# A graph attention layer and a graph network with pair features: the first weight turned alone, the other weights after the first graph, and the layer norm of thirty graphs placed between the steps of the last two

## The reference, cut to what matters

```python
# x (32, 256, 128), adj (32, 256, 256); layer norms are without gain and bias
def _L0_gnn_ref(x, adj, W, b, a):            # H = 4 heads of D = 32
    h = (x @ W + b).reshape(Bb, Nn, H, D)
    e_i = jnp.einsum('bnhd,d->bnh', h, a_i)
    e_j = jnp.einsum('bnhd,d->bnh', h, a_j)
    e = e_i[:, :, None, :] + e_j[:, None, :, :]
    e = jnp.where(e > 0, e, 0.2 * e)
    e = jnp.where(adj[..., None] > 0, e, NEG)
    attn = jax.nn.softmax(e, axis=2)
    return jnp.einsum('bijh,bjhd->bihd', attn, h).reshape(Bb, Nn, H * D)
...
x = _layernorm(x + _L0_gnn_ref(x, adj, ...), axis=-1)
x = _layernorm(x + _L1_gnn_ref(x, adj, W1, ..., Wg, ..., Wt, ...), axis=-1)
```

## Time and profile before

| | before |
|---|---|
| time of the runs | median 2240.56 us of 3 (2239.26 to 2241.79) |
| profiled execution | 2237.45 us, its span 2235.6 us |
| DVE busy | 2090.6 us, 94% |
| ACT busy | 2093.6 us, 94% |
| PE busy | 1977.0 us, 88% |
| granted PE clock, mean | 0.984 of full |

### The profile page before, as it was taken

One profiled execution on the slowest core, in us unless ns is written; L12 is line 12 of the kernel. 1 busy time (PEld: TensorE's weight loads), 2 busy tenths in 40 slices (PEclk: granted clock), 3 DMA queues, 4 the chain that ended last, 5 costly groups with the idle time before them and its releaser, 6 DMA issues.

```text
span 2235.6 us, 35341 instructions
## 1 busy us (share of the span) xinstructions
PE 1977.0 (88%) x13059; PEld 781.5 (35%) x13059; DVE 2090.6 (94%) x2519; ACT 2093.6 (94%) x2764; POOL 54.6 (2%) x50
## 2 busy tenths in 40 slices
PE   6888878989989898989899898986999999999986
PEld 4666533333333333333333333332222222222225
DVE  6999789999999999999999999998899999999976
ACT  4999879999999999999999999996999999999976
POOL 0000000000000000000000000000000000111000
PEclk9999989999999999999999999998999999999997
DMA  4112144445444444444454444444999999999972
GB/s 127 51 51 58 30 155 183 174 182 193 179 177 182 180 176 189 186 184 173 184 190 181 178 178 187 174 184 170 370 348 359 365 369 361 372 357 367 362 258 76
DMA packets 221281, 470.52 MB, mean 210 GB/s; under 512 B 52344, under 2 KB 143288, under 8 KB 196536
## 3 DMA queue, kind: packets, MB, share of 16 engines
q1 hardware_dynamic: 220048, 467.91, 56.4%
q10 hardware_dynamic: 1064, 0.36, 0.1%
HBM read 254.25 MB, written 213.91 MB: 209 GB/s over the span
## 4 chain that ended last, share of the span: by engine, by line
ACT 38%; DVE 22%; issue 21%; PE 4%; DMA 2%; SPq 1%; POOL 0%; ACTq 0%; POOLq 0%; DVEq 0%
DVE diff L1334 10%; ACT hcopy L625 9%; ACT habs L625 9%; ACT yt L630 8%; ACT diff L613 7%; DVE diff L1339 4%; ACT banks L635 2%; PE banks L863 1%; ACT diff L615 1%; ACT habs L657 1%; DVE adjt L1351 1%; DMA hcopy<-kept 1%; DVE small L1364 1%; DVE rows L1179 1%; DMA diff<-kept 1%
## 5 line engine op out<-in xcount | busy, mean ns | idle before, releaser
L863 PE MATMUL banks<-diff,w1t 128*64 128x512 f32 x5136 | 1206.6, 603 | 128.6 <-ACT hcopy L625 57.0
L1194 DVE TENSOR_TENSOR diff<-ring 128x2048 f32<-128x2048 f32 x352 | 802.9, 2289 | 42.0 <-PE banks L863 42.0
L863 PEld LDWEIGHTS banks<-diff,w1t 128*64 128x64 f32 x5136 | 346.5, 137 | 862.5 <-issue 792.8
L1208 DVE TENSOR_SCALAR diff<-diff 128x2048 int32<-128x2048 int32 x354 | 418.5, 1221 | 0.0
L1334 DVE TENSOR_TENSOR diff<-ring 128x2048 f32<-128x2048 f32 x128 | 296.1, 2313 | 3.5 <-PE banks L863 3.5
L613 ACT ACTIVATE diff<-banks 128x2048 f32<-128x2048 f32 x128 | 238.5, 1863 | 2.7 <-PE banks L878 2.7
L630 ACT ACTIVATE yt<-habs,par 128x2048 f32<-128x2048 f32 x96 | 192.4, 2005 | 3.1
L630 ACT ACTIVATE yt<-hcopy,par 128x2048 f32<-128x2048 f32 x96 | 192.4, 2005 | 3.1
L625 ACT ACTIVATE hcopy<-banks 128x1024 f32<-128x1024 f32 x192 | 193.7, 1018 | 0.6 <-PE banks L863 0.6
L625 ACT ACTIVATE habs<-banks 128x1024 f32<-128x1024 f32 x192 | 193.7, 1018 | 0.3 <-PE banks L863 0.3
L878 PE MATMUL banks<-pick,yt 32*128 32x256 f32 x2560 | 184.9, 403 | 1.0 <-ACT ring L596 1.0
(11 more groups left out here) (213 smaller groups left out, 1852.1 us busy)
## 6 DMA issues: line engine op xcount, KB each, us to landing
kept<-hcopy SPq DMA_DIRECT2D x192, 512.0 KB, 2.9
kept<-habs SPq DMA_DIRECT2D x192, 512.0 KB, 2.9
hcopy<-kept SPq DMA_DIRECT2D x78, 1024.0 KB, 6.9
diff<-kept SPq DMA_DIRECT2D x76, 1024.0 KB, 7.0
habs<-kept SPq DMA_DIRECT2D x38, 1024.0 KB, 7.0
yt<-xrows SPq DMA_DIRECT2D x512, 40.0 KB, 2.0
adjt<-in_adj_dram SPq DMA_DIRECT2D x32, 256.0 KB, 2.9
diff<-in_x_dram SPq DMA_DIRECT2D x32, 128.0 KB, 2.1
```

The costliest lines, as they stand in the source:

```text
L863: last = nc.tensor.matmul(dst[half * O:(half + 1) * O, bank * BANK:(bank + 1) * BANK], w1t[:, :], src[:, m * BANK:(m + 1) * BANK], start=T ...
L1194: v.tensor_tensor(shaped(diff[:, c % ND, :]), xj, xi_, ALU.subtract).then_inc(sub_done, 1)
L1208: v.tensor_scalar(bits, bits, ABS_BITS, None, ALU.bitwise_and).then_inc(abs_dve, 1)
```

## The change

Three things. **Start:** W0 alone is turned first, and `v` goes to the PSUM bank 6 instead of bank 2, so that PE can turn the first x without waiting for DVE's copy of `v`; SP takes over one column of `a` and the loads of W1, Wg and Wt; these are turned (`turn_weights`) and copied (`keep_weights`) after the first graph's scores. SP no longer waits for W1, Wg and Wt ahead of the rows' load. **End:** moments, square root and reciprocal of the 60 tiles of graphs 0 to 29 are taken while graphs 30 and 31 drain, groups 0 to 4 are scaled there, and the last four tiles get moments of their own. **Place:** `em` and `pt` lie further back in `ring`, since its front is now filled while they are in use, and the turned groups go to PSUM banks 0, 1, 6 and 7.

```diff
-        em = [ring[:, q * 2048:(q + 1) * 2048] for q in range(2)]
-        pt = ring[:, 8192:8192 + NT * H * N].rearrange("p (t h n) -> p t h n", t=NT, h=H)
+        em = [ring[:, 6144 + q * 2048:6144 + (q + 1) * 2048] for q in range(2)]
+        pt = ring[:, 10240:10240 + NT * H * N].rearrange("p (t h n) -> p t h n", t=NT, h=H)
...
+        lnp = [banks[:, i * BANK:(i + 1) * BANK] for i in (0, 1, 6, 7)]
...
-            sp.wait_ge(w_loaded, 64)
-            sp.wait_ge(a_loaded, 48)
+            sp.dma_start(wraw[0:O, 0, :], W1).then_inc(w_loaded, 16)
+            sp.dma_start(wraw[:, 1, :], Wg).then_inc(w_loaded, 16)
+            sp.dma_start(wraw[:, 2:4, :], Wt.rearrange("o (k c) -> o k c", k=2)).then_inc(w_loaded, 16)
+            sp.wait_ge(w0_loaded, 16)
+            sp.wait_ge(a_loaded, 32)
+            sp.wait_ge(b0_loaded, 16)
             sp.wait_ge(b0b_loaded, 16)
...
+            def row_deviations(k):
+                act.wait_ge(ln_var, k + 1)
+                part = slice(60, 64) if k else slice(0, 60)
+                nc.scalar.activation(rstd[:, part], rstd[:, part], ACT.Sqrt).then_inc(ln_sqrt, 1)
...
             for b in range(-2, B + 1):
...
                     bend_scores(b + 1)
+                if b == B - 1:
+                    row_deviations(0)
+                if b == B:
+                    to_ring(1)
                 if 0 <= b - 1 < B:
                     copy_sums(b - 1)
...
                     copy_weights(b, 0)
+                if b == B - 1:
+                    to_ring(0)
+            for g in range(2, TILES // 4 - 1):
+                to_ring(g)
+                if g == 5:
+                    row_deviations(1)
+            to_ring(TILES // 4 - 1)
...
-            pe.wait_ge(v_copied, 1)
+            def turn_weights():
+                pe.wait_ge(w_loaded, 48)
...
+                if b == 0:
+                    pe.wait_ge(v_copied, 1)
...
+            def keep_weights():
+                dve.wait_ge(wt_ready, 1)
+                tw = ps[2]
+                v.tensor_copy(w1t[:, :], tw[:, P:P + O])
+                v.tensor_copy(wgt[:, :], tw[:, 2 * P:3 * P])
+                v.tensor_copy(wtt[:, 0, :], tw[:, 4 * P:5 * P])
+                v.tensor_copy(wtt[:, 1, :], tw[:, 5 * P:6 * P]).then_inc(w_kept, 1)
...
+                if b == -1:
+                    keep_weights()
+                if 0 <= b - 1 < B - 2:
+                    if b == 1:
+                        dve.wait_ge(rows_loaded, 64)
+                    add_rows(b - 1)
+            row_moments(0, slice(0, 60), 60)
+            row_scales(0, slice(0, 60))
+            norm_rows(0)
+            add_rows(B - 2)
+            row_statistics(B - 2)
+            for g in range(1, 5):
                 norm_rows(g)
+            add_rows(B - 1)
+            row_statistics(B - 1)
+            row_moments(1, slice(60, 64), 64)
+            for g in range(5, TILES // 4 - 1):
+                norm_rows(g)
+            row_scales(1, slice(60, 64))
+            norm_rows(TILES // 4 - 1)
```

More of the change, by code:

```diff
@@ L169, in gnn_pair_kernel @@
         yp = ps[3][:, BANK + 256:2 * BANK]
+        w0_loaded = sem("w0_loaded")
+        w0_turned = sem("w0_turned")
+        b0_loaded = sem("b0_loaded")
         w_loaded = sem("w_loaded")
+        w_kept = sem("w_kept")
         ident_zero = sem("ident_zero")
@@ L524, in _ @@
         def _(act):
[L526 to L533, removed]
+            act.dma_start(acols[:, 0:1], bass.AP(a0.tensor, a0.offset, [[0, H], [1, DH], [1, 1]])).then_inc(a_loaded, 16)
+            act.dma_start(w0raw, W0).then_inc(w0_loaded, 16)
+            act.dma_start(b0col, b0.rearrange("(n a) -> n a", a=1)).then_inc(b0_loaded, 16)
             act.dma_start(b0b, b0.rearrange("(a n) -> a n", a=1).to_broadcast([P, C])).then_inc(b0b_loaded, 16)
@@ L586, in _ @@
                     copy_weights(b, 0)
[L589 to L597, removed]
-            for g in range(TILES // 4):
-                to_ring(g, g % 4)
+                if b == B - 1:
[5 more added lines that the diff above has]
+            to_ring(TILES // 4 - 1)
             def column(n):
@@ L795, in transpose_weights @@
                     pe.wait_ge(pt_copied, 2 * b + t)
+                else:
+                    pe.wait_ge(w_kept, 1)
                 for jt in range(NT):
@@ L828, in sums_to_rows, with transpose_rows @@
                 last.then_inc(rowt_ready, 1)
+            def transpose_rows(g):
+                pe.wait_ge(ln_row, g + 1)
+                if g >= 4:
+                    pe.wait_ge(ln_copied, g - 3)
+                for t in range(4):
+                    last = nc.tensor.transpose(lnp[g % 4][:, t * P:(t + 1) * P], rows[:, 4 * g + t, :], ident[:, :])
+                last.then_inc(ln_tr, 1)
             for b in range(-2, B + 1):
-                if 0 <= b - 1 < B:
+                if 0 <= b - 1 < B - 1:
                     transpose_weights(b - 1, 1)
@@ L840, in _ @@
                     transpose_weights(b, 0)
+                if b == B:
+                    transpose_rows(2)
                 if 0 <= b - 1 < B:
@@ L844, in _ @@
                     project_x(b + 2)
-            def transpose_rows(g, q):
-                pe.wait_ge(ln_row, g + 1)
-                if g >= 4:
-                    pe.wait_ge(ln_copied, g - 3)
-                for t in range(4):
-                    last = nc.tensor.transpose(ps[q][:, t * P:(t + 1) * P], rows[:, 4 * g + t, :], ident[:, :])
-                last.then_inc(ln_tr, 1)
-            for g in range(TILES // 4):
-                transpose_rows(g, g % 4)
+                if b == -1:
+                    turn_weights()
+                if b == B - 1:
+                    transpose_rows(0)
+                if b == B - 1:
+                    transpose_weights(b, 1)
+                    transpose_rows(1)
+            for g in range(3, TILES // 4):
+                transpose_rows(g)
             pe.wait_ge(ln_copied, TILES // 4)
@@ L1175, in norm_rows, with row_scales @@
+            def row_scales(k, part):
+                dve.wait_ge(ln_sqrt, k + 1)
+                v.reciprocal(rstd[:, part], rstd[:, part]).then_inc(ln_ready, 1)
+                dve.wait_ge(ln_ready, k + 1)
             def norm_rows(g):
```

111 lines of the change are left out of this document (53 added, 58 removed).

## The result

| | before | after |
|---|---|---|
| runs | 2240.36 us median of 6 (2236.19 to 2243.58) | 2229.68 us median of 6 (2224.88 to 2229.95) |
| ratio | | 0.9960, 95% interval 0.9944 to 0.9976 |
| profiled execution | 2237.45 us, span 2235.6 | 2224.88 us, span 2223.0 |

The change is faster, by 9.0 us by the ratio (5.4 to 12.5) and 10.7 us by the medians.

What follows compares the result with a forecast made beforehand. DVE and ACT were both 94% busy, so gains came only from idle time at the attention layer's start and drain: 1.7 + 5.4 = 7.1 us off the 2240.56 median gives 2233.5 us, range 2230.5 to 2237.

Steps and rivals of the forecast that it cites:

- rival 4: Attention steps: moved `em` and `pt` lengthen each of 32 steps, so the kernel is slower, say 2246 us; chance 0.05.
- The end, 5.4 us: Drain and layer norm: work moved into DVE's waits starts the pair stage at 298.05 instead of 303.50, 5.4 us gained.
- DVE's wait for graph 31: Drain: DVE, free since 280.9, waits 1 us for graph 31's rows at 281.95.
- the delay of graph 31: Drain: PE's transposes ahead of graph 31's weighted sums make its rows reach DVE 0.65 us late.
- the small moments: Drain: seven moments of 4 columns for the last tiles on DVE, taken as 1.2 us.
- The table load: Drain on ACT: 1.28 us, hidden by the wait before `copy_sums`, with 0.5 us to spare.
- rival 2: Drain: the table load is not covered and graph 30's chain is late by 0.8 us, giving 2234.3 us; chance 0.07.
- The start, 1.7 us: Attention layer's start: an earlier rows' load brings graph 2's x at 30.2 instead of 31.90, 1.7 us gained.
- I take 7.2, so the rows' load starts at 7.2: SP's queue at the start: b0's landing lets the rows' load start at 7.2 us instead of 8.91.
- the seventeen loads behind it follow at the pace of the queue and of the DMA engines: SP's queue: loads behind the rows' load pass its earlier start on to graph 2's x, 1.7 us.
- the loads' chain ends last: Start, at graph 2: the loads, not the set-up, set its beginning; the set-up has over 5 us of room.
- The pair stage and all behind it are passed the shift of their own start: From the pair stage on: everything moves by the shift of its start, with no further gain or loss.

Runs made afterwards that it cites:

- e3: Only the end of the change (layer norm, drain, moved `em` and `pt`) on the kernel before, set-up as before; ratio to before 0.9968 (0.9956 to 0.9979).
- e2: Only the start of the change (set-up edits) on the kernel before, layer norm as before; ratio to before 0.9998 (0.9987 to 1.0009).
- e12: Changed kernel with the additions of e9 and e11 together; ratio to before 0.9939 (0.9921 to 0.9956), median 2221.34 us.
- e10: Kernel before with SP's thirteen parameter loads put behind the loads of x and adj; ratio to before 0.9975 (0.9964 to 0.9985).
- e6: Changed kernel with SP's thirteen parameter loads put behind all attention-layer loads of x and adj; ratio to before 0.9948 (0.9935 to 0.9961).
- e1: Kernel before, unedited, profiled a second time in one run; PE took 1.93 us over graph 30's sums, pair stage started at 301.32 us.
- e5: Changed kernel, unedited, profiled a second time with more rounds; ratio to before 0.9964 (0.9952 to 0.9977).
- e9: Changed kernel with parameter loads last and graph 2's x ahead of the rows' load; ratio to before 0.9921 (0.9906 to 0.9937), median 2220.98 us.
- e11: Changed kernel with unread identity transposes on PE late in the layer norm and at the pair stage's start; ratio to before 0.9950 (0.9937 to 0.9963).
- e7: Changed kernel with SP waiting only for W0, not a, b0 and b0 broadcast, before the rows' load; ratio to before 0.9963 (0.9951 to 0.9976).
- e4: Kernel before with 48 unread identity transposes on PE ahead of the old layer norm's first transposes; ratio to before 0.9998 (0.9988 to 1.0009).

## Why the prediction was right, and where it was off

**The place and the direction** were right: two stretches of idle time, both used, and the rest of the kernel at its old pace (a step takes 7.72 us before and 7.71 after, and from graph 2 to graph 31 it is 224.36 us before and 224.39 in e3, so the moved `em` and `pt` cost nothing: rival 4 fell). That the number came near is in part luck: the start was taken 1.0 us too high, and 1.2 us at the pair stage's start were not in the sum; the two cancel.

**The end, 5.4 us.** The sum was made of the right pieces. Against its own rows: DVE's wait for graph 31 1.03 for 1.0; the delay of graph 31 0.65 in e3, exactly as summed; from `add_rows` of graph 31 to the pair stage 15.69 for the 16.10 of the sum. The mis-sized term is the small moments, 0.78 us (281.16 to 281.94) where I took 1.2. What the end gives depends on PE's clock at the drain. From graph 31's first instruction to the pair stage the table has three pairs of an old and a new end with the same dip: 43.10 and 37.16 us (before and e3), 42.91 and 36.94 (e2 and e12), 42.73 and 36.75 (e10 and e6), so 5.9 to 6.0 us are gained. At full clock it is 41.49 in e1 and 36.66 in four of the changed kernels (after, e5, e9, e11): 4.8 us. The 5.4 of the sum lies between the two.

**The table load.** The forecast had it covered with 0.5 us to spare. That holds at the lower clock (e3: root done at 273.1, sums copied at 273.64 right behind PE). At full clock PE has the sums at 269.9, and ACT copies them at 270.99: the switch is exposed for 1.1 us, which is the difference between 5.9 and 4.8. That is rival 2's mechanism, not by a longer switch but by a faster PE: my cover was 3.57 us of PE work, which lasts 1.93 in other executions. The switch itself took 1.28 us and the root started at once (269.54 to 270.83), as in the earlier trace rows; the drain of 1.38 us that the Trainium skill adds (ScalarE: Activation LUTs, section "What ACT_TABLE_LOAD costs") did not show here either, its 1283 ns did, so 1.28 us is the price here.

**The start, 1.7 us.** Wrong in size. It gave about 0.7 us: SP started the rows at 8.33 and 8.41, and at 8.63 in e2, against 8.91 and 9.18; and graph 2 starts at 35.46 in the mean of the five traces with the new start and the old order of loads (34.82 to 35.96; e7 left out), at 36.19 in the four with the old one (36.04 to 36.55). The failed step is "I take 7.2, so the rows' load starts at 7.2". The column b0 was there at 7.60, as in the worse case that the sum had named, and b0 broadcast, issued at 2.94, was waited for until 8.3: it took 5.2 us to land, not the 3.5 that it had taken in the kernel before, issued at 5.30 behind seven loads (not six). Two causes fit. One is SP's weights beside it: e7 shows that more data on SP's queue does hold these 64 KB back (6.7 us). The Trainium skill (DMA: Bandwidth & Descriptors, section "Queues, rings and completion order") states that a DMA's semaphore increment lands only behind every earlier write of the same DMA engine, across its queues; that rule would hold b0 back too, and the landing fits it. The other is that it is now issued 2.4 us earlier, while x and adj of graphs 0 and 1 are still on their way (adj issued at 2.09 and 3.07, 5.1 us to landing). For this one speaks the column b0, which took 5.1 us in both kernels, with SP's weights (2.46 to 7.60) and without them (2.63 to 7.77). No run left SP's weights away alone, so this stays open. The step behind it, "the seventeen loads behind it follow at the pace of the queue and of the DMA engines", does not pass an earlier start on either: e7 started 2.5 us earlier and gained 0.3. That the loads' chain ends last was right, and e6 and e9 show it.

**What was not in the sum.** "The pair stage and all behind it are passed the shift of their own start" failed: the pair stage's first 14.3 us took 12.3 to 13.6 in all seven traces with the new end and no filling, 14.3 in all five with the old one. What shortens them is PE's clock: with the old end it falls to its lower level within the first product, with the new one the first product still runs at full clock (1.15 us for sixteen matmuls against 1.7 to 2.1), and e11 shows what the whole dip costs. Why the new end puts off the dip is not settled: e4 rules out the wait ahead of the layer norm alone, and over the last groups PE's work is nearly the same in both (four transposes in 0.66 us, with a wait of 0.37 before them; with the new end 0.58 before the last group's). With 1.2 us here in the mean of the seven, 5.9 at the end and 0.7 at the start the pieces come to 7.8 us at the lower clock at the drain, and to 6.7 at full clock. The runs say 8.1 and 9.0, each with an interval of 2.8 us or more. The first trace pair's 10.2 holds another 2.4 us of luck: PE's clock at graph 2 and the step behind it (1.2), at the drain (0.5) and at the pair stage's start (0.7).

## What to carry to other kernels

When two chains meet at one point, the one that ends last takes back whatever the other gains: here 3.3 us that the set-up had gained by the end of graph 1 came to nothing at graph 2, until thirteen small loads, needed only behind the pair stage, over 1000 us later, left the queue ahead of its x. A load that an engine will wait for belongs ahead of a big one in the same queue; starting that queue 2.5 us earlier gained 0.3 here, putting the load first gained 2.7 at graph 2 (e9 against e6). And a cover made of PE work is only as long as PE's clock makes it: work it out at both levels. The same end is worth 5.9 us where the dip comes and 4.8 where it does not.

## What the runs showed of the hardware

The same kernel's PE clock fell at the drain in one execution and not in the next (3.57 and 1.93 us for the same 32 matmuls), in eight of the fourteen traces in all. Up to the pair stage that is worth 1.2 to 1.6 us with the old end (42.73 to 43.10 us from graph 31's first instruction, against 41.49) and 0.1 to 0.5 us with the new one (36.75 to 37.16, against 36.66). At or soon after the pair stage's start the clock fell in every trace except the two where PE was given unread transposes for the waits there (e11, e12), also where it had been at full level for 17 us before (e4). Filling those waits shortened that stretch by 1.3 to 2.1 us in the trace. Starting 4 MB of loads 2.5 us earlier brought what stands behind them forward by only 0.3 us: four issues took 12.04 us instead of 9.88. A load of 64 KB in ACT's queue, issued at 2.94, took 5.2 us to land, and 6.7 when that big load started 2.5 us earlier on SP's queue. An ACT table load of 1283 ns started 0.02 us behind the instruction ahead of it (269.54, the exponentials having ended at 269.52), and the root 0.01 us behind the load.
